# Cross attention on one core: the setup in another order and with other homes for its weights

## The reference

```python
query, keyt, valt = hidden_states @ Wq, enc @ Wk, enc @ Wv
hs = _mha(query, keyt, valt)                      # 8 heads of 80
ca_q1 = einsum('btc,th->bch', ca, Wq_ca)[:, indices, :]
ca_hs1 = _mha(ca_q1, residual, residual)
ca_q2 = ca_hs1 @ Wq
ca_k2, ca_v2 = ca @ Wk_ca, ca @ Wv_ca
ca_hs2 = _mha(ca_q2, ca_k2, ca_v2)
out = (hs + ca_hs2) @ Wout + b_out + residual
```

## Time and profile before

| | |
|---|---|
| median of 3 runs | 1541.65 us (1541.1 to 1544.61) |
| the profiled execution | 1540.79 us, its span 1539.0 us |
| granted clock over the span | 0.996 |
| PE busy | 1499.8 us (97%) |
| DVE, ACT busy | 791.1 us (51%), 620.0 us (40%) |
| the chain of work that ended last | PE 91%, DVE 4%, ACT 2%, issue 2% |
| first products of x in batch 0 | 53.7 us after the span's start |

### The profile page before, as it was taken

How to read it: one execution, slowest core, us unless ns; L and a number is a source line. 1 busy time by engine, 2 the same in 40 slices (tenths; PEclk the granted TensorE clock), 3 DMA queues, 4 the chain that set the end, 5 groups by cost and what they waited for, 6 DMA issues and landing times.

```text
span 1539.0 us, 24550 instructions
## 1 busy us (share of the span) xinstructions
PE 1499.8 (97%) x10306; PEld 1247.5 (81%) x10306; DVE 791.1 (51%) x1595; ACT 620.0 (40%) x1310; POOL 2.8 (0%) x12
## 2 busy tenths in 40 slices
...
GB/s 241 205 136 35 3 54 70 55 114 26 89 170 130 1 16 48 66 111 54 35 111 182 88 1 20 82 28 156 18 35 155 180 38 1 20 95 57 61 18 43
DMA packets 46680, 117.28 MB, mean 76 GB/s; under 512 B 3661, under 2 KB 5317, under 8 KB 45019
## 3 DMA queue, kind: packets, MB, share of 16 engines
...
## 4 chain that ended last, share of the span: by engine, by line
PE 91%; DVE 4%; ACT 2%; issue 2%; DMA 0%; SPq 0%
PE ps_w L508 46%; PE ps_s L508 19%; PE ps_t L508 16%; PE ps_t L518 5%; PE ps_w L518 3%; DVE unit_max L1311 2%; ACT work L1124 1%; PE ps_s L518 1%; ACT ot L1038 0%; DMA y_all<-in_L_xattn_Wv_ca_dram 0%; DVE ca_mat L1327 0%; DVE ot L1423 0%; ACT ot L1107 0%; DVE xt_l L1337 0%; ACT work L1021 0%
## 5 line engine op out<-in xcount | busy, mean ns | idle before, releaser
L508 PE MATMUL ps_w<-wo_h,ot 128*128 128x320 f32 x1280 | 310.4, 314 | 0.6 <-DVE ot L1423 0.6
L1311 DVE TENSOR_REDUCE unit_max<-ps_s 128x1 f32<-128x512 f32 x384 | 240.6, 683 | 53.1 <-PE ps_s L508 52.2
L1094 ACT ACTIVATE work<-ps_s,neg_max 128x150 f32<-128x150 f32 x512 | 152.5, 403 | 223.4 <-DVE neg_max L1369 223.4
L508 PEld LDWEIGHTS ps_w<-wo_h,ot 128*128 128x128 f32 x1280 | 220.3, 188 | 0.9 <-DVE ot L1423 0.9
L508 PE MATMUL ps_w<-wo_l,ot 128*128 128x320 f32 x640 | 197.4, 308 | 0.0
L508 PEld LDWEIGHTS ps_w<-v_all,work 120*128 120x128 f32 x1280 | 170.3, 190 | 3.0 <-issue 2.5
L508 PE MATMUL ps_w<-v_all,work 120*128 120x162 f32 (+1 forms) x1280 | 171.3, 288 | 0.0
L1365 DVE TENSOR_REDUCE neg_max<-ps_s 128x6 f32<-128x900 f32 x64 | 70.1, 1095 | 165.2 <-PE ps_s L508 165.2
L508 PE MATMUL ps_s<-keys_h,qt_h 128*128 128x300 f32 (+1 forms) x448 | 140.0, 313 | 0.0
L508 PE MATMUL ps_s<-keys_h,qt_l 128*128 128x300 f32 (+1 forms) x448 | 131.5, 294 | 0.0
L508 PE MATMUL ps_s<-keys_l,qt_h 128*128 128x300 f32 (+1 forms) x448 | 131.1, 293 | 0.0
...
## 6 DMA issues: line engine op xcount, KB each, us to landing
xc<-in_x_dram SPq DMA_DIRECT2D x32, 1280.0 KB, 6.5
...
xt_l<-xt_all SPq DMA_DIRECT2D x12, 1280.0 KB, 5.6
y_all<-in_L_xattn_Wk_dram SPq DMA_DIRECT2D x4, 960.0 KB
y_all<-in_L_xattn_Wv_dram SPq DMA_DIRECT2D x4, 960.0 KB
...
xc<-in_L_xattn_Wq_dram SPq DMA_DIRECT2D x1, 1600.0 KB, 10.5
```

Source lines behind the costliest of these rows:

```text
L508: return nc.tensor.matmul(out, lhs, rhs, start=start, stop=stop, skip_group_check=True)
L1094: return nc.scalar.activation(probs[:, h * KEYS:(h + 1) * KEYS], ps_s[:, bank, c * KEYS:(c + 1) * KEYS], exp, bias=neg_max[:, s % 2, h:h + ...
L1311: v.tensor_reduce(unit_max[:, a, n, q:q + 1], bank, AX_X, ALU.max).then_inc(max_free, 1)
```

## The change

- **Homes.** Wk_ca and Wv_ca get homes of their own for the setup (`wk_ca` in `work`, `wv_ca` in `xc`). SP no longer waits for `kv2_full` before it loads Wk, Wv and the context of batch 0.
- **DVE.** The bias steps and the shared value columns come ahead of kv2. The mask products `k2_bd` and `v2_bd` come ahead of Wq's low part. The high part of Wout is made by ACT (`wo_high`), the low part by DVE after batch 0's base columns. The split of vw2 is made in two halves, after Wout's.
- **PE.** vw2 is made after batch 0's keys, in `ps_w` and `ps_t`. Batch 0's context is turned straight after m2. Four matmuls whose result is not read stand ahead of the keys. `vw2_ready` is waited for ahead of the first turned piece of x.
- **SP.** x's chunks 0 and 1 are loaded after `wo_ready` and `vw2_full`, and the stores of vw2 come behind both loads.
- **ACT.** `pick_all` is stored after Wout's high part. `vw2_out` is waited for ahead of the first `copy_g`.

```diff
 UNREAD = 4
-UNREAD_SUMS = 3
+UNREAD_SUMS, UNREAD_SETUP = 3, 4
 ALL_RUNS = range(7)
...
 wq_t = [xc[:, KT + j, :] for j in range(3)] + [o_norm[:, :], probs_t[:, 5:10, :].rearrange("p a b -> p (a b)")]
+wk_ca = work[:, 0:CT * HID].rearrange("p (k n) -> p k n", k=CT)
+wv_ca = xc[:, KT:KT + CT, :]
 vw2_h, vw2_l = ot_h[:, 0, :], ot_l[:, 0, :]
...
     sem("m2_taken"), sem("gyw_first"), sem("gyw_in"))
+wo_high = sem("wo_high")
 su_turned, kv2_full, vw2_full, m2_full = sem("su_turned"), sem("kv2_full"), sem("vw2_full"), sem("m2_full")
...
 piece_bank = {piece: ps_t[:, n % 2, :] for n, piece in enumerate(PIECES)}
+vw2_banks = [ps_w[:, 2, 0:HALF], ps_t[:, 0, 0:HALF]]
 score_banks = [ps_w[:, 0:2, 0:CAD], ps_t[:, 0:2, 0:CAD]]
...
     sp.dma_start(wqca_in, Wq_ca).then_inc(su_small_in, 16)
-    sp.dma_start(wk, Wk_ca.rearrange("(k p) n -> p k n", p=P)).then_inc(su_ca_in, 16)
-    sp.dma_start(wv, Wv_ca.rearrange("(k p) n -> p k n", p=P)).then_inc(su_ca_in, 16)
+    sp.dma_start(wk_ca, Wk_ca.rearrange("(k p) n -> p k n", p=P)).then_inc(su_ca_in, 16)
+    sp.dma_start(wv_ca, Wv_ca.rearrange("(k p) n -> p k n", p=P)).then_inc(su_ca_in, 16)
     sp.dma_start(stage_w, Wq.rearrange("(k p) n -> p k n", p=P)).then_inc(su_wq_in, 16)
...
-        if b == 0:
-            sp.wait_ge(kv2_full, 1)
-        else:
+        if b:
             sp.wait_ge(s2_ready, START + b)
...
             sp.dma_start(gyw_all.rearrange("b p n -> p b n"), gyw_raw.rearrange("p b n k -> p b (n k)")).then_inc(gyw_out, 16)
-            sp.wait_ge(vw2_ready, 1)
-            for r, part in enumerate((vw2_h, vw2_l, vw2_h)):
-                sp.dma_start(vw2_all[r], part.bitcast(F32)).then_inc(vw2_out, 16)
             sp.wait_ge(wo_ready, 1)
+            sp.wait_ge(vw2_full, 1)
             load_x(0, 0)
...
             load_x(1, 1)
+            sp.wait_ge(vw2_ready, 1)
+            for r, part in enumerate((vw2_h, vw2_l, vw2_h)):
+                sp.dma_start(vw2_all[r], part.bitcast(F32)).then_inc(vw2_out, 16)
         else:
...
     for c in range(CT):
-        for r, (w, lo, hi) in enumerate(((wk, 0, CAD), (wv, 0, CAD), (wk, CAD, HID), (wv, CAD, HID))):
+        for r, (w, lo, hi) in enumerate(((wk_ca, 0, CAD), (wv_ca, 0, CAD), (wk_ca, CAD, HID), (wv_ca, CAD, HID))):
             last = mm(ps_w[32 * r:32 * (r + 1), 2, 0:hi - lo], ca_t[:, c, :], w[:, c, lo:hi], c == 0, c == CT - 1)
...
-    pe.wait_ge(su_wout_in, 16)
-    pe.wait_ge(v2_ready, 1)
-    for half in range(2):
-        for j in range(KT):
-            last = mm(ps_t[:, half, 0:HALF], v2_bd[:, j, :], stage_w[:, j, half * HALF:(half + 1) * HALF], j == 0, j == KT - 1)
-    last.then_inc(vw2_full, 1)
-    pe.wait_ge(vw2_ready, 1)
-
     def turn_x(k, kt, bank, full):
...
+    pe.wait_ge(v2_ready, 1)
     turn_ctx(0)
+    pe.wait_ge(wq_ready, 1)
+    for n in range(UNREAD_SETUP):
+        mm(ps_w[:, 1, :], wq_h[:, n, 0:P], wq_h[:, n, 0:CHUNK], True, True)
     for b in range(B):
...
+        if b == 0:
+            pe.wait_ge(su_wout_in, 16)
+            for half in range(2):
+                for j in range(KT):
+                    last = mm(vw2_banks[half], v2_bd[:, j, :], stage_w[:, j, half * HALF:(half + 1) * HALF], j == 0, j == KT - 1)
+            last.then_inc(vw2_full, 1)
+
         pe.wait_ge(cst_base, b + 1)
...
                 pe.wait_ge(xc_in[0], 16 * (b * XC_LOADS + 1))
+                pe.wait_ge(vw2_ready, 1)
                 turn_x(0, 0, piece_bank[("x", 0)], gx_turned)
...
         nc.scalar.activation(wq_t[j], src[:, 0:HID], copy).then_inc(wq_copied, 1)
-    act.dma_start(pick_all, c_pick).then_inc(pick_out, 16)
...
     take_ctx(0)
+    act.wait_ge(su_wout_in, 16)
+    nc.scalar.activation(wo_h[:, :, :], stage_w, copy).then_inc(wo_high, 1)
+    act.dma_start(pick_all, c_pick).then_inc(pick_out, 16)
     for b in range(B):
...
             act.wait_ge(stored[k], START + 16 * b * (SLOTS // 2))
-        if b == 0:
-            act.wait_ge(vw2_out, 16 * 3)
         for m in range(GX):
...
                 q0_highs(i - 2)
+            if b == 0 and m == KT + 2:
+                act.wait_ge(vw2_out, 16 * 3)
             if i and kt == 2:
...
+    dve.wait_ge(su_misc_in, 16 * 5)
+    for r in range(2):
+        v.tensor_copy(v_all[:, r, V_SHARED[0]:V_SHARED[-1] + 1, :, DH], rem_of[:, :, :])
+
+    rows = slice(3 * HT, 3 * HT + 2)
+    steps.done(v.tensor_copy(vw2_b[rows, :], bias_in))
+    steps.done(v.tensor_tensor(bias_tmp, bias_in, vw2_b[rows, :], ALU.subtract))
+    steps.done(v.tensor_scalar(bias_tmp, bias_tmp, hi_lo[rows, 1:2], None, ALU.mult))
+    steps.done(v.scalar_tensor_tensor(bias_in, vw2_b[rows, :], hi_lo[rows, 0:1], bias_tmp, ALU.mult, ALU.add))
+    v.tensor_copy(vw2_b[rows, :], bias_in)
+
     dve.wait_ge(kv2_full, 1)
...
     steps.done(v.tensor_copy(wq_h[:, :, :], stage_w))
-    v.tensor_tensor(wq_l[:, :, :], stage_w, wq_h[:, :, :], ALU.subtract).then_inc(wq_ready, 1)
     dve.wait_ge(kv2_turned, 1)
-    dve.wait_ge(su_misc_in, 16 * 5)
     for a, (dst, full) in enumerate(((k2_bd, kv2_ready), (v2_bd, v2_ready))):
...
-    for r in range(2):
-        v.tensor_copy(v_all[:, r, V_SHARED[0]:V_SHARED[-1] + 1, :, DH], rem_of[:, :, :])
-
-    rows = slice(3 * HT, 3 * HT + 2)
-    steps.done(v.tensor_copy(vw2_b[rows, :], bias_in))
-    steps.done(v.tensor_tensor(bias_tmp, bias_in, vw2_b[rows, :], ALU.subtract))
-    steps.done(v.tensor_scalar(bias_tmp, bias_tmp, hi_lo[rows, 1:2], None, ALU.mult))
-    steps.done(v.scalar_tensor_tensor(bias_in, vw2_b[rows, :], hi_lo[rows, 0:1], bias_tmp, ALU.mult, ALU.add))
-    v.tensor_copy(vw2_b[rows, :], bias_in)
+    v.tensor_tensor(wq_l[:, :, :], stage_w, wq_h[:, :, :], ALU.subtract).then_inc(wq_ready, 1)
...
-    dve.wait_ge(vw2_full, 1)
-    halves = lambda a: a.rearrange("p (a n) -> p a n", a=2)
-    steps.done(v.tensor_copy(halves(vw2_h), ps_t[:, 0:2, 0:HALF]))
-    v.tensor_tensor(halves(vw2_l), ps_t[:, 0:2, 0:HALF], halves(vw2_h), ALU.subtract).then_inc(vw2_ready, 1)
-    dve.wait_ge(su_wout_in, 16)
-    steps.done(v.tensor_copy(wo_h[:, :, :], stage_w))
-    v.tensor_tensor(wo_l[:, :, :], stage_w, wo_h[:, :, :], ALU.subtract).then_inc(wo_ready, 1)
+    by_rung = cst[:, :, :, :].rearrange("p c a (r k) -> p c a r k", r=GROUPS)
+
+    def base_columns(b):
-    for b in range(B):
         dve.wait_ge(enc_full, b + 1)
...
         steps.close()
-        by_rung = cst[:, :, :, :].rearrange("p c a (r k) -> p c a r k", r=GROUPS)
         for a in range(PHASES):
...
+    base_columns(0)
+    dve.wait_ge(wo_high, 1)
+    v.tensor_tensor(wo_l[:, :, :], stage_w, wo_h[:, :, :], ALU.subtract).then_inc(wo_ready, 1)
+    dve.wait_ge(vw2_full, 1)
+    for half in range(2):
+        cols = slice(half * HALF, (half + 1) * HALF)
+        steps.done(v.tensor_copy(vw2_h[:, cols], vw2_banks[half]))
+        last = v.tensor_tensor(vw2_l[:, cols], vw2_banks[half], vw2_h[:, cols], ALU.subtract)
+    last.then_inc(vw2_ready, 1)
+
+    for b in range(B):
+        if b:
+            base_columns(b)
+
         dve.wait_ge(k_full, b + 1)
```

More of the change, by code:

```diff
@@ L450, in _ @@
                     sp.dma_start(gyw_all.rearrange("b p n -> p b n"), gyw_raw.rearrange("p b n k -> p b (n k)")).then_inc(gyw_out, 16)
+                    sp.wait_ge(wo_ready, 1)
+                    sp.wait_ge(vw2_full, 1)
+                    load_x(0, 0)
+                    sp.wait_ge(gyw_out, 16)
+                    load_x(1, 1)
                     sp.wait_ge(vw2_ready, 1)
@@ L453, in _ @@
                         sp.dma_start(vw2_all[r], part.bitcast(F32)).then_inc(vw2_out, 16)
-                    sp.wait_ge(wo_ready, 1)
-                    load_x(0, 0)
-                    sp.wait_ge(gyw_out, 16)
-                    load_x(1, 1)
                 else:
@@ L1196, in _ @@
             v.tensor_copy(wqca_t, ps_s[:, 2, n:n + KT * TOK].rearrange("p (k n) -> p k n", k=KT)).then_inc(su_turned_ready, 1)
-            dve.wait_ge(kv2_full, 1)
-            v.tensor_copy(kv2_rows[0:64, :], ps_w[0:64, 2, 0:CAD])
-            v.tensor_copy(kv2_rows[64:P, 0:HID - CAD], ps_w[64:P, 2, 0:HID - CAD]).then_inc(kv2_copied, 1)
-            dve.wait_ge(su_wq_in, 16)
-            steps.done(v.tensor_copy(wq_h[:, :, :], stage_w))
-            v.tensor_tensor(wq_l[:, :, :], stage_w, wq_h[:, :, :], ALU.subtract).then_inc(wq_ready, 1)
-            dve.wait_ge(kv2_turned, 1)
-            dve.wait_ge(su_misc_in, 16 * 5)
-            for a, (dst, full) in enumerate(((k2_bd, kv2_ready), (v2_bd, v2_ready))):
-                for j in range(KT):
-                    at = j % CT * P + 32 * (a + 2 * (j // CT))
-                    mask = head_of[:, j, :].unsqueeze(1).unsqueeze(3).broadcast_to([P, B, HEADS, TOK])
-                    src = ps_s[:, 2, at:at + B * TOK].rearrange("p (b t) -> p b t", b=B).unsqueeze(2).broadcast_to([P, B, HEADS, TOK])
-                    last = v.tensor_tensor(dst[:, j, :].rearrange("p (b h t) -> p b h t", b=B, h=HEADS), src, mask, ALU.mult)
-                last.then_inc(full, 1)
+            dve.wait_ge(su_misc_in, 16 * 5)
```

12 lines of the change are left out of this document (added).

## The result

The changed kernel takes 1535.76 us, the median of 5 runs (1533.53 to 1535.86), against 1543.65 for the kernel before in the same set (lowest 1541.1). One of the five runs of the kernel before took 5000.67 us; it has no part in the ratio, and without it the median is 1542.65. The ratio is 0.9951 with a 95% interval of 0.9935 to 0.9967, so 7.6 us less, between 5.1 and 10.0. Forecast were 1534.0 and 7.7 us less, in a range of 1531.8 to 1538.2. The profiled execution took 1535.76 us, its span 1534.0, against 1540.79 and 1539.0.

What follows compares the result with a forecast made beforehand. PE, busy 1499.8 of 1539.0 us, was taken as the bound, winnable only where it waits or runs at half clock. Setup terms -2.7 -2.7 -1.8 +0.2 -1.7 +1.0 = -7.7 us gave 1534.0 us, range 1531.8 to 1538.2.

Steps and rivals of the forecast that it cites:

- vw2's split: Setup, before the context turns: context turned straight behind m2, no longer waiting 1.78 us for DVE's split; -1.8 us.
- m2's start: Setup: mask products ahead of Wq's low part let m2 start at 18.9 instead of 21.6; -2.7 us.
- the clock in m2: Setup: with the pause before it 0.9 us, m2 runs at full clock instead of 5.36 us at half; -2.7 us.
- the unread matmuls: Setup, ahead of the keys: four matmuls cost +0.2 us; keys at full clock behind them bring -1.7 us.
- signs of being wrong: Forecast wrong if m2 starts later than 20, or x's turn is at 43 and the end moved under 6 us.
- Rival 1: Clock still falls at m2's start, 3.4 to 5.4 us at half; 1535.7 to 1536.7 us, chance 0.25.
- Wout and the high part: Setup: Wout lands at 29.3, ACT's high part takes 2.9 us, `wo_ready` at 35.7 just ahead of `vw2_full` at 36.4.
- x, +1.0: Setup's end: x's first chunk, issued at 36.4, lands at 42.4; PE comes at 41.5 and waits, +1.0 us.
- The stores of vw2: Issued at 38.2 behind 2560 KB of x, in DRAM by 48, before ACT's first copy of g near 56.7; no cost.
- rival 2: x's first chunk comes later, through Wout's 9.0 us load or `pick_all` still moving; 1535.5 to 1537.4 us, chance 0.12.
- Rival 5: Setup: early loads of Wk, Wv and context delay the weights PE waits for; slower, 1545.1 us, chance 0.02.
- rival 3: Behind 54 us: half-clock stretches of 3.4 us cost up to 1.7 each by batch; 1532.3 to 1539.1 us, chance 0.07.

Runs made afterwards that it cites:

- second profile: Changed kernel run and profiled once more, nothing altered, against the kernel before: profiled 1533.27 us, median 1534.96, ratio 0.9947.

## Why the prediction was right

The time is inside the range, and the mechanism is the one forecast: m2 lost most of its pause and all of its half clock, the pause for vw2's split went, the keys ran at full clock, and the first chunk of x became the new wait. Single terms missed by up to 0.9 us, and the misses nearly cancel: m2's start fell 0.9 us short of its term and the clock in m2 0.1 us, while x and the unread matmuls cost 0.6 us less than forecast and vw2's split brought 0.2 us more. That the sum came within 0.3 us is in part luck.

One of the prediction's own signs of being wrong came in the first profile: the turn of x stood near 43 (43.26) and the end had moved by 5.0 us, less than 6. In the second profile it did not: 42.63, and 7.5 us. What lay behind it was no step of the setup, but for the most part 3.4 us more at half clock in batch 2.

- **m2's start, -2.7:** -1.8 in the first profile, -2.6 in the second (19.03). The mechanism was right; the step left out that kv2 and the first turns of Wq may run at half clock, and for how long, which moved all by 0.7 us between the two profiles. In the trace of before kv2 took 3.49 us and looked like a fixed price.
- **The clock in m2, -2.7:** m2 took 5.65 us instead of 8.22 up to the next group: -2.6. Rival 1 did not come in any kernel whose m2 started within a microsecond of Wq's turns. The Trainium skill (TensorE: Matmul & The Clock Gate, Part 4: PE-mode transpose) has transposes not count for the clock. The runs speak against it. With 12 unread products from the start PE had nothing but turns and idle time for 6.4 us, from kv2's end at 12.8 to m2, and PEclk stayed 1.00. With the low part ahead of the masks it held for 8 us behind kv2's end, at 14.5, and fell at 22.6. In the kernel before it fell at 20.1, 6.1 us behind kv2's end and 2.1 us into the pause behind the turns. How much a turn counts, these runs don't show.
- **vw2's split, -1.8:** the pause is gone, and vw2 takes 5.38 us up to the next group instead of 7.33: -2.0.
- **The unread matmuls, +0.2 and the cover for the keys' clock:** the cost was 0, and the keys' -1.7 came as forecast (5.60 to 3.88 us). The reason given for it is in doubt: in the one profile without the unread matmuls the keys keep the clock too.
- **Wout and the high part:** 29.3 and 2.9 us forecast, 29.8 and 2.87 measured. `wo_ready` and `vw2_full` came in the order forecast.
- **x, +1.0:** +0.6. It landed 5.8 us after its issue, and PE came there 5.7 us after `cst`. The term did not follow from the prediction's own figures: vw2's end at 36.4 and 5.5 us give 41.9, not 41.5, and the other terms put the turn at 42.0, against a landing at 42.4. So +0.4 to +0.5 was due, with the turn near 42.4 instead of 42.8. With it the sum would have been -8.3.
- **The stores of vw2:** no cost in the changed kernel, as forecast; with ACT's wait for them at its old place the time behind the turn is 2.3 us more, and with the stores ahead of x the turn is 4.3 us later.
- **The rivals on the queue:** `pick_all`, which by rival 2 might still be moving at 37, had landed by 35.6. Rival 5 did not come: kv2 began at 10.60 instead of 10.49, and Wq landed at 14.6 instead of 14.45. Its working has two slips that change no term of the sum: 14.0 + 4.9 is 18.9 (19.4 starts from Wq's landing at 14.45), and Wq's 1600 KB in 4.1 us give 9.0 us for 3520 KB and 5.5 for 2151, not 8.1 and 4.9, which no row shows.
- **The sum:** -7.7 forecast, -7.4 at the first turn of x, -7.6 by the ratio. The first profile lost 2.4 of it again, 1.7 by 3.4 us more at half clock, of rival 3's kind. Rival 3 let the change decide which batch has such a stretch, and that can't be read from it: two profiles of one program, 0.63 us apart at the turn, have them in different batches.
